# A recommender tower on one core: the order in which all engines take their work is replaced as a whole

## What is computed

```
e = stack([tbl_f[ids[:, f]] for f in range(40)], axis=1)     # (2048, 40, 32)
z = einsum('bke,kef,bkf->bk', e[:, I, :], W, e[:, J, :])     # 780 pairs I < J, W (780, 32, 32)
h = concatenate([z, dense_ctx], axis=1)                       # (2048, 796)
h = maximum(h @ W_top1 + b_top1, 0)                           # 512
h = maximum(h @ W_top2 + b_top2, 0)                           # 256
y = h @ W_top3                                                # (2048, 1)
```

## Time and profile before

| | us |
|---|---|
| median of 3 runs (lowest, highest) | 1132.43 (1129.46, 1133.22) |
| span of the profiled execution, first to last instruction | 1130.1 |
| TensorE matmuls busy | 875.4 (77%), 7232 records |
| VectorE busy | 540.3 (48%) |
| GpSimd busy | 412.3 (36%) |
| ScalarE busy | 327.1 (29%) |

### The profile page before, as it was taken

How to read it: one execution, slowest core, us unless ns; L and a number is a source line. 1 busy time by engine, 2 the same in 40 slices (tenths; PEclk the granted TensorE clock), 3 DMA queues, 4 the chain that set the end, 5 groups by cost and what they waited for, 6 DMA issues and landing times.

```text
span 1130.1 us, 16792 instructions
## 1 busy us (share of the span) xinstructions
PE 875.4 (77%) x7232; PEld 201.8 (18%) x7232; DVE 540.3 (48%) x510; ACT 327.1 (29%) x243; POOL 412.3 (36%) x436
## 2 busy tenths in 40 slices
PE   4322358788779995886895789779889787899998
PEld 1000012121112220121121112112112111122223
DVE  3100067364345660452380447337245264688884
ACT  4001047553246380032260134127244000000002
POOL 6777341533353137324517151451624604000000
PEclk8555598887578895886796788989779788899999
DMA  4100044201001020100101002010010102011010
GB/s 155 32 14 13 12 145 127 63 7 52 9 11 53 12 72 13 44 16 18 38 22 41 5 10 75 9 47 4 12 34 8 39 3 58 8 39 29 1 36 3
DMA packets 30489, 39.24 MB, mean 35 GB/s; under 512 B 11376, under 2 KB 19200, under 8 KB 30160
## 3 DMA queue, kind: packets, MB, share of 16 engines
q1 hardware_dynamic: 14880, 25.59, 7.7%
q0 software_dynamic: 13824, 7.11, 4.3%
q10 hardware_dynamic: 1712, 5.48, 1.4%
HBM read 21.93 MB, written 0.07 MB: 19 GB/s over the span
## 4 chain that ended last, share of the span: by engine, by line
PE 65%; another core or an unknown queue 17%; issue 11%; DVE 3%; ACT 2%; SPq 1%; DMA 1%; DVEq 0%; ACTq 0%
PE t_ps L857 27%; PE z_ps L881 18%; PE x_ps L898 10%; PE x_ps L806 7%; PE x_ps L911 2%; SPq L543 1%; DVE prod L727 1%; ACT one_hot L602 1%; PE t_ps L911 1%; DVE one_hot L689 1%; PE t_ps L898 1%; PE t_ps L829 0%; DVE z_sb L673 0%; ACT one_hot L605 0%
## 5 line engine op out<-in xcount | busy, mean ns | idle before, releaser
L727 DVE TENSOR_TENSOR prod<-t_ps,e_t 128x1024 f32<-128x1024 f32 x392 | 459.4, 1213 | 425.2 <-remote 300.6
L558 POOL DMA_INDIRECT rows<-cold_tables,idx x432 | 412.1, 954 | 550.1 <-DVE e_t L734 420.2
L857 PE MATMUL t_ps<-e_t,w_sb 32*64 32x512 f32 x3120 | 362.0, 658 | 73.8 <-issue 53.6
L881 PE MATMUL z_ps<-prod,select 128*32 128x512 f32 x1560 | 243.5, 639 | 21.7 <-issue 21.0
L602 ACT ACTIVATE one_hot<-hot_sb,row_number 128x2048 bf16<-128x2048 f16 (+1 forms) x75 | 140.6, 1875 | 110.3 <-remote 87.4
L898 PE MATMUL x_ps<-z_sb,w_sb 128*32 128x512 f32 x704 | 131.1, 635 | 24.4 <-issue 22.5
L605 ACT ACTIVATE one_hot<-one_hot 128x2048 bf16<-128x2048 bf16 (+1 forms) x75 | 134.3, 1791 | 2.4
L857 PEld LDWEIGHTS t_ps<-e_t,w_sb 32*64 32x64 f32 x3120 | 74.6, 136 | 323.0 <-issue 221.6
L806 PE MATMUL x_ps<-one_hot,tables 128*32 128x512 bf16 x1194 | 97.8, 402 | 27.3 <-issue 22.6
L806 PE MATMUL t_ps<-one_hot,tables 128*32 128x512 bf16 x198 | 45.3, 501 | 92.1 <-issue 87.9
L689 DVE TENSOR_SCALAR one_hot<-hot_sb,row_number 128x2048 bf16<-128x2048 f16 (+1 forms) x47 | 33.9, 744 | 133.2 <-remote 130.0
(11 more groups left out here) (33 smaller groups left out, 98.6 us busy)
## 6 DMA issues: line engine op xcount, KB each, us to landing
e_t<-e_t SPq DMA_DIRECT2D x64, 128.0 KB
e_t<-e_t SPq DMA_DIRECT2D x112, 64.0 KB
rows<-cold_tables,idx POOLq DMA_INDIRECT x432
hot_sb<-hot_ids SPq DMA_DIRECT2D x11, 512.0 KB, 3.6
w_sb<-w_lay ACTq DMA_DIRECT2D x1, 1792.0 KB, 7.0
z_sb<-hot_tables SPq DMA_DIRECT2D x4, 320.0 KB, 5.1
w_sb<-w_lay ACTq DMA_DIRECT2D x1, 1216.0 KB
w_sb<-w_lay ACTq DMA_DIRECT2D x1, 896.0 KB, 4.6
```

Of the source, the lines that this page charges most:

```text
L558: pool.indirect_dma_start(out=rows[:, slot, span, :], out_offset=None, in_=table, in_offset=bass.IndirectOffsetOnAxis(ap=idx[:, n, span:sp ...
L727: nc.vector.tensor_tensor(prod[:, u % PROD_SLOTS, 0:banks, :], t_ps[:, at:at + banks, :], by, ALU.mult).then_inc(mult_done, 1)
L857: mm = nc.tensor.matmul(t_ps[cols, at + n, :], w_sb[part, b, cols], e_t[part, e_slot(k, of[side]), :], start=True, stop=True)
L881: mm = nc.tensor.matmul(z_ps[E * q:E * q + E, :], select[:, E - PER - PER * s:2 * E - PER - PER * s], prod[:, (u + q // 2) % PROD_SLOTS, q ...
```

## The change

The string `ORDER` is replaced by another with the same letters in the same numbers, with one exception: of the 122 one-hots, 75 were made by ScalarE (O) and 47 by VectorE (o); now they are 72 and 50. No other line of the program changes.

```diff
@@ -162,14 +162,14 @@
 ORDER = """
-pippppipphpoohoOppoohopphpohOppohpoophphpopohhhooOhpoohpohhopohphhpotopOhhohhhpgpoophhhphOhrhoohhoooppghhhOooh
...
+pppppippopooppOppihohpohhphhoopoopoppOopphhoohoOhOpppohohhopphhhohohhOoohphhpgohpohOhprhohhpohohpoophhhooOhoOg
...
 """
```

More of the change, by code:

```diff
@@ L164 @@
 ORDER = """
-pippppipphpoohoOppoohopphpohOppohpoophphpopohhhooOhpoohpohhopohphhpotopOhhohhhpgpoophhhphOhrhoohhoooppghhhOooh
[L166 to L172, removed]
+pppppippopooppOppihohpohhphhoopoopoppOopphhoohoOhOpppohohhopphhhohohhOoohphhpgohpohOhprhohhpohohpoophhhooOhoOg
+hhghhotOrOgOrhgrghhgrgOrtrgrhghOhgrgOhorgrOrghOgtrOhgrrgrOghOrgrgOhOOhgrtrghrghOhgrhOogrrghhgrgOrrtgOhrghhgrgt
+rOrOOghrgOhhgorrgrhOghrgOhhgrOorghrghhgOrgorhgrrOghOrgOhrghrghrtg11g1rg1OrOg11grrtgO1rg1rtOg11g1rgr1grrghrgrOh
+grhgorhgrOhhgrOohgohrgthhrgo11g1O1trOgO11grOrrghhgrrohOgrhogrhOhghOhgrhgtrrgrhg1rg1rgOtO1rg1rg11grrg2rg2rg2rg2
+rgO2rg2Org22ghrgrhOghrghrghhgrOrogrOthgrhg1rgo11grrgO1rOgO11grrg1rtgt11gr11gr1gOrrgohhOghrhgOOrhtgrrgOhrgrhgOr
+hhghrgrO1g11tgrO1ogr11gr33grrtOgOhrghrohghohrOghrohghrhgrhgr1g11gr1g11grr2gr2grrgr2tgt2rg22g2rgrgr2g3rgrrg3rg1
+rg1grg1rg1gr1gr1grtrg11gr1tgrrgr1g11grrgr1g1rgr1gt11gr1grrg11g1rtg1rgrg1rgr1grrg22gtr2g2rgrrgr2g22grrg2rg11gr1
+gr1tgr1grrg11grrg1rgr1g11gr1gr1g1rg1rgr1gr3gr3g1r1r1111112222222233
 """
```

## The result

The changed kernel takes 1145.28 us in the median of 4 runs (1142.09 to 1150.54), the kernel before on the same chip 1130.95 us (1126.30 to 1133.22): ratio 1.0115, 95% interval 1.0068 to 1.0163, so 14 us slower. The profiled execution took 1142.09 us with a span of 1140.1 us. The time lies inside the range, 0.7 us under its upper end, and not within 0.3% of before, where I had put it; the rival nearest to it is "chains at full price", 1142 us. The profiled execution is the fastest of the four, so the spans differ by 10 us and the medians by 14.

A forecast was written before the change was run, and what follows sets the result against it. The kernel was taken to be bound by TensorE's work plus the gathers' holds, one after the other. Start +1.1, chains +4 and balance -4 summed to +1.1 us, a 1131.2 us span and 1133.5 us median; range 1121 to 1146.

The forecast's parts named there:

- chains at full price: Rival, near turns: 4.5 us for each of two added chains, start +5.0, balance at most -4; 1142 us, chance 0.29.
- What bounds the kernel: Whole kernel: TensorE's work (611 us) plus gathers' holds, one after the other; fine order of letters hardly matters.
- The start: From 139.5 us to the third turn: turn 3.9 us sooner, TensorE 5.0 us more to do later; net +1.1 us.
- balance between the gathers: Chunk 0, three one-hots from ScalarE to VectorE: a smoother order wins -4 us, bounds 0 and -19.
- The tail: After the last gather: TensorE runs without pause at full clock, same kinds of steps before and after; 0 us.
- Chains: Near turns make a gather follow another without gap: pairs rise from two to four, 2 us each, +4 us.
- The upper bound of 4.5 us: Price of one chain from whole stretches: two pairs, mean 37.3 us, against 2 x 16.4 = 32.8 us.
- the pairs: Two double stretches of chained gathers in the kernel before, costing 36.8 and 37.9 us, mean 37.3.
- that stand alone: Four unchained gathers of the kernel before, costing 15.6, 18.8, 16.8 and 14.5 us, mean 16.4 us each.
- 19 us of room: Chunk 0: a stretch costs 20.2 us, 3.8 over the mean; five such hold at most 19 us to win.
- The clock alone: Rival: a gather's cost is mostly TensorE's clock falling, so two more chains save 8.4 us; 1121 us, chance 0.07.
- no difference: Whole kernel: the forecast of 1133.5 us, range 1129 to 1137, not distinguishable from before; chance 0.40.

The follow-up runs named there:

- the first half: New string only up to the 13th turn (letter 417), old string behind it: 1132.22 against 1132.83 us for the kernel before, ratio 1.0000.
- the second half: Old string up to the 13th turn, new string behind it, against the kernel before: 1145.70 us, ratio 1.0119.
- the kernel with single marks: Old string, but each DMA of the gathers behind the first six waits for its own product count, against the kernel before: 874.62 us, ratio 0.7677.

## Why the prediction was right or wrong

**What bounds the kernel: right.** The sum of TensorE's work and of holds by gathers was the reading on which all rested. The runs bear it out: without touching TensorE's work, pauses between the same DMAs take away 23% of the time. That the fine order hardly matters was right for the first half, 1.0000, and too sweeping for the second.

**The start: right in kind.** +1.1 us was forecast together with a balance of -4; the first half as a whole gives 0.0 with 3.6 us either way, so that even the -2.9 of the two together is neither borne out nor excluded. The turn came 2.6 us sooner instead of 3.9. The tail, put at nothing, has 1090 records from 960 to 1060 us after, beside 1108 in the window before.

**Chains: right.** Their number went from two to four as counted from products between turns, each second gather passes nine or ten records, and the price taken, 2 us, measures 1.9. The upper bound of 4.5 us came from a base of only four gathers, and one of these was no gather alone (below). The twelve gathers of the kernel before that are neither in a pair, nor next to a gap of 5 or 6 us, nor the last cost 17.4 us by the same rates, and against them the pairs, 37.3, cost 2.5 more. That was in the trace.

**What failed is that the sum had nothing for short gaps between gathers, a term of +5.1 us as measured; and the term "balance between the gathers", -4 us, which hid the chains in the sum, is borne out by nothing.** I had two kinds of gather, alone and chained, and gave all that stand alone 16.4 us. There is a third: the two with a gap of 5 to 6 us. One of them, from 809.50 to 860.80 us, was among my four gathers "that stand alone" and the cheapest, 14.5 us; the other I had left out. Moving the two turns costs 5.1 us. The new string has none of these gaps, a loss that I could have read from the list of products between turns: the 6 products ahead of the 18th and of the 20th turn are 14 and 28 in the new string. The balance that I credited brought nothing that could be seen: the first half, where it was to act, is at 1.0000, though -4 us is not beyond the noise once the start's +1.1 stands beside it. Its 19 us of room were too many as well: the stretch of 20.2 us in the earlier trace rows is the dearest of the five that begin between 151.7 and 316.7 us, which cost 18.3 us on average, and 17.9 after the change.

**The rival nearest to the result had the right size by luck.** It puts 9 us on chains and 5 us on the start, less 4 of balance. Measured are 3.9 us of added chains, 5.1 us of lost gaps, and 0 in the first half; 4 us are left, within the noise. That the time still lies in the range is luck as well: the range was set by the bounds of start and chains, and more than a third of the loss is in neither. The clock alone, 1121 us, is refuted: added chains make the kernel slower.

The chance of 0.40 for no difference was too high: the terms of the second half pointed one way, and the -4 us that cancelled them rested on no row of that half.

## What to carry to other kernels

Where one engine's loop issues many small gathers, look at the other engines' records in windows inside such a stretch before the balance of instructions is touched: the share of busy time hides it, since a crawling TensorE still counts as busy for a quarter to a half of the time (29.58 of 115 us, 9.31 of 20). If it crawls after some 7 us, break the gathers into the smallest pieces, with pauses tied to the progress of the work, and keep the pieces from running together; here that is worth 258 us, where a new order of everything moved 14. And in a search over orders, what triggers such a stretch is the letter that counts: four of 837 letters carried three quarters of the loss.

## What the runs showed of the hardware that I had not expected

A gather of GpSimd lets TensorE run for some 7 us (75 records in 7.4 us), then passes about one TensorE record in 2 us (9 or 10 in 20 us), with TensorE waiting for nothing that the trace shows. After a pause of 5 or 6 us the next gather has most of its opening again (56 and 63 records in 7.4 us); after 0.3 us it has none. Single DMAs with pauses of 1 to 3 us after every two to five of them leave 3966 records in 400 us at a granted clock of 0.99 (nearly always the upper level, 2.4 GHz), beside 211 DMAs. GpSimd's timeline of the kernel with single marks shows such pieces:

```profile
401.01 0.94 POOL L573 DMA_INDIRECT rows<-cold_tables,idx  x1 [2.89 <-DVE prod L742]
402.26 0.95 POOL L573 DMA_INDIRECT rows<-cold_tables,idx  x1 [0.30 <-issue]
403.51 0.94 POOL L573 DMA_INDIRECT rows<-cold_tables,idx  x1 [0.30 <-issue]
404.76 0.96 POOL L573 DMA_INDIRECT rows<-cold_tables,idx  x1 [0.30 <-issue]
408.53 0.94 POOL L573 DMA_INDIRECT rows<-cold_tables,idx  x1 [2.82 <-DVE prod L742]
```

What makes TensorE crawl was not found. The Trainium skill ("Runtime: NRT & Kernel Launch", Instruction fetch mechanics) says that an engine fetches its instructions ahead in blocks through DMAs of its own, and that this is mostly hidden. A fetch that is not hidden while gathers run would be a guess at the cause, but the traces speak against it. The DMA view has queues that it calls instruction; before, one of them moved 57 packets over the whole program. In all four second gathers after the change it shows none, only the gather's own queue, here from 932 to 952 us:

```profile
q0 software_dynamic: 512, 0.26, 9.0%
```

And TensorE's records stand there one by one, several of them 2.80 us apart:

```profile
939.79 1.01 PE L857 MATMUL t_ps<-e_t,w_sb 32*64 32x512 f32 x1 [1.79 <-issue]
942.59 1.01 PE L857 MATMUL t_ps<-e_t,w_sb 32*64 32x512 f32 x1 [1.79 <-issue]
945.39 1.01 PE L857 MATMUL t_ps<-e_t,w_sb 32*64 32x512 f32 x1 [1.79 <-issue]
```

If blocks came late, a whole block would wait at once and then run; here each instruction waits by itself. Nor is it the amount of data: 0.26 MB in 20 us is 13 GB/s, and in the 28.8 us ahead of the first turn the DMAs move 210 GB/s while TensorE passes 372 records. The cause stays open.
